# Sums of squares of an RMS norm by plain fp32 matmuls, and one weight group's sums by DMA, in a two-block FFN kernel

## The reference, cut to what matters

```python
def cond(x):        # LoRA of rank 16, one adapter per sequence, added to each of the three products
    act = silu(lora(x @ W_gate.T)) * lora(x @ W_up.T)        # 512 -> 1376
    return lora(act @ W_down.T)                              # 1376 -> 512

def ffn(y):
    nx = y * rsqrt(mean(y * y, -1) + 1e-5) * ln_w            # the norm
    return (silu(nx @ gate_w.T) * (nx @ up_w.T)) @ down_w.T  # 512 -> 1792 -> 512

out = x + ffn(cond(x))                                       # x: 8 sequences of 128 tokens, 512 features, fp32
```

## Time and profile before

| | us |
|---|---|
| median of 3 runs (395.55 to 397.08) | 396.54 |
| profiled execution, its own time | 396.24 |
| its span, first to last instruction | 394.5 |
| PE busy | 387.4 |
| DVE busy | 334.4 |
| ACT busy | 252.0 |
| POOL busy | 23.8 |

### The profile page before, as it was taken

How to read it: one execution, slowest core, us unless ns; L and a number is a source line. 1 busy time by engine, 2 the same in 40 slices (tenths; PEclk the granted TensorE clock), 3 DMA queues, 4 the chain that set the end, 5 groups by cost and what they waited for, 6 DMA issues and landing times.

```text
span 394.5 us, 5731 instructions
## 1 busy us (share of the span) xinstructions
PE 387.4 (98%) x1954; PEld 321.4 (81%) x1954; DVE 334.4 (85%) x478; ACT 252.0 (64%) x389; POOL 23.8 (6%) x25
## 2 busy tenths in 40 slices
PE   9999999999999999999899999999999999999997
PEld 5899888888888888788668888888888888888885
DVE  4799979585869889999899887878787869899994
ACT  5879886857746699994646656464646494484740
POOL 6300000000013011011100000000000000000000
PEclk9999999999999999999999999999999999999999
DMA  7540243311293997524400221313130316005112
GB/s 272 178 138 0 83 130 102 123 53 55 86 248 95 261 301 159 142 33 93 135 0 1 78 83 53 108 53 111 61 120 29 98 49 234 21 0 202 53 53 107
DMA packets 17694, 41.46 MB, mean 105 GB/s; under 512 B 2562, under 2 KB 5634, under 8 KB 17666
## 3 DMA queue, kind: packets, MB, share of 16 engines
q1 hardware_dynamic: 13792, 33.89, 25.6%
q0 software_dynamic: 2752, 5.37, 8.0%
q10 hardware_dynamic: 1122, 1.84, 1.3%
HBM read 33.75 MB, written 2.10 MB: 91 GB/s over the span
## 4 chain that ended last, share of the span: by engine, by line
PE 92%; DVE 5%; issue 1%; ACT 1%; DVEq 0%
PE bank L1631 51%; PE bank L2006 17%; PE bank L1886 10%; PE bank L1803 3%; PE bank L1849 3%; PE bank L1838 3%; PE bank L1641 3%; PE bank L1744 1%; PE bank L1797 1%; DVE nx L1353 1%; DVE xs L1074 1%; PE bank L1900 1%; ACT xs L535 1%; DVE wx L1074 1%; PE bank L2015 0%
## 5 line engine op out<-in xcount | busy, mean ns | idle before, releaser
L1631 PE MATMUL bank<-xs,ws 128*128 128x512 f32 x840 | 196.0, 390 | 1.3 <-DVE xs L1074 1.2
L1631 PEld LDWEIGHTS bank<-xs,ws 128*128 128x128 f32 x840 | 156.3, 188 | 34.5 <-ACT bank L535 1.6
L535 ACT ACTIVATE xs<-act 128x512 fp32r<-128x512 f32 (+1 forms) x72 | 49.5, 709 | 22.7 <-DVE act L1292 7.5
L1074 DVE TENSOR_TENSOR xs<-act,xs 128x512 fp32r<-128x512 f32 (+1 forms) x66 | 49.7, 766 | 3.4 <-ACT xs L535 2.8
L1074 DVE TENSOR_TENSOR ws<-wraw,ws 128x256 fp32r<-128x256 f32 (+2 forms) x45 | 30.0, 668 | 13.3 <-ACT ws L535 13.2
L535 ACT ACTIVATE bank<-bank 128x512 f32<-128x512 f32 x34 | 19.4, 578 | 34.0 <-PE bank L1631 32.4
L535 ACT ACTIVATE mu<-bank 128x512 f32<-128x512 f32 x44 | 26.1, 596 | 22.6 <-PE bank L1631 16.0
L2006 PE MATMUL bank<-xs,vs 128*128 128x512 f32 x168 | 38.2, 389 | 0.0
L2006 PEld LDWEIGHTS bank<-xs,vs 128*128 128x128 f32 x168 | 31.5, 188 | 6.5
L1074 DVE TENSOR_TENSOR ws<-wsum,ws 128x1024 fp32r<-128x1024 f32 x20 | 24.5, 1224 | 10.8 <-ACT ws L535 10.7
L535 ACT ACTIVATE ws<-wraw 128x256 fp32r<-128x256 f32 (+2 forms) x44 | 26.9, 615 | 6.9 <-PE bank L1631 3.3
(11 more groups left out here) (149 smaller groups left out, 494.5 us busy)
## 6 DMA issues: line engine op xcount, KB each, us to landing
wraw<-wgu_in SPq DMA_DIRECT2D x22, 512.0 KB, 3.3
wdr<-vs_in SPq DMA_DIRECT2D x7, 512.0 KB, 3.5
wraw<-vj_in SPq DMA_DIRECT2D x3, 896.0 KB, 4.6
act<-act POOLq DMA_DIRECT2D x4, 512.0 KB, 9.9
down_w_raw<-wc_in SPq DMA_DIRECT2D x3, 640.0 KB, 4.1
down_w_sums_raw<-wc_in SPq DMA_DIRECT2D x3, 640.0 KB, 5.1
xa<-xT_in SPq DMA_DIRECT2D x4, 256.0 KB, 4.1
xa<-xT_in ACTq DMA_DIRECT2D x2, 512.0 KB, 5.0
```

The lines of the kernel that those rows point to most:

```text
L535: return nc.scalar.activation(out_ap, in_ap, ACT.Copy, scale=scale)
L1074: return nc.vector.tensor_tensor(out_ap, raw, v32(part), ALU.subtract)
L1631: ins = mm(z[:, :], w_slot(j)[:, w, s, k * P:(k + 1) * P], xs[:, c, r, k, :], start=(start and k == 0 and s == 0 and r == 0), stop=(k == 1 ...
```

## The change

1. **Sums of squares without a split.** `sum_squares` reads `sqr` itself, with ones and the squares both taken as plain fp32, one matmul in place of two. `sum_hi`, `sum_lo`, `square_hi` and the split in `last_square` go. In half 1 both sums stand behind q1(9), no longer inside it. What waited for a split waits for the matmul (`s_nm`).
2. **Sums of set 11 by DMA.** DVE's `sums(11)` goes. SP gets `load_base(11)`, POOL `two_w(11)` and `more_w(11)`. `load_base(11)` waits for the sixth activation DMA, `T4_23`. The sums of set 12 move to a buffer in `xsum_f[:, 3]`, and `load_base(12)` waits for product 22's first low part.
3. **Work moved.** `hi_b(11)` and `lo_b(11)` move from before t1's operands to behind `square(2)` on ACT and behind `lo_c(CT1, 2)` on DVE. `copy_u3` moves ahead of t1's first operand and weights. `hi_b(12)` and `lo_b(12)` move from before the norm of half 0 to behind t1's operand of the second block (`hi_x(T_SLOT[0])`, `lo_t(1, 0)`). `scale(2)` and `scale(3)` move ahead of half 1's squares. `norm(1)`, `scale(6)` and `scale(7)` move ahead of `lo_a(13)`.

```diff
         def sums_done(j):
-            if G1 + 1 < j < G1 + 4:
-                return s_wadd, 32 * (j - G1 - 1)
-            return s_wsum, 3 * (j - 1 - (2 if j > G1 + 1 else 0))
+            if G1 < j < G1 + 4:
+                return s_wadd, 32 * (j - G1)
+            return s_wsum, 3 * (j - 1 - (3 if j > G1 else 0))
...
             def load_base(j):
-                sp.wait_ge(s_wblo, j - 2)
-                sp.dma_start(wsum[:, :, :], wbase_in[j - G1 - 2].rearrange("p (a m) -> p a m", a=4)).then_inc(s_wbase, 16)
+                if j == G1 + 2:
+                    sp.wait_ge(s_clo, KC * C22 + 2)
+                elif j == G1 + 3:
+                    sp.wait_ge(s_wblo, j - 3)
+                    sp.wait_ge(s_wbase, 32)
+                else:
+                    sp.wait_ge(s_wblo, j - 2)
+                sp.dma_start(wsum_of(j), wbase_in[j - G1 - 1].rearrange("p (a m) -> p a m", a=4)).then_inc(s_wbase, 16)
 
             load_w(G1 + 2)
+            sp.wait_ge(*t_added(T4_23))
+            load_base(G1 + 1)
+            load_w(G1 + 3)
             load_base(G1 + 2)
-            load_w(G1 + 3)
             load_base(G1 + 3)
...
-            for j in range(G1 + 2, G1 + 4):
+            for j in range(G1 + 1, G1 + 4):
                 two_w(j)
                 more_w(j)
...
-            hi_b(G1 + 1)
             hi_w10(1)
+            for i in range(2):
+                copy_u3(i)
             hi_c(CT1, 0)
             hi_w(CT1, (s_cw_add, 16))
-            for i in range(2):
-                copy_u3(i)
...
             square(2)
+            hi_b(G1 + 1)
             hi_c(CT1, 2)
...
-            sum_hi(0)
             hi_c(C22, 1)
             hi_c(C22, 2)
-            hi_b(G1 + 2)
             rsqrt(0)
...
-            sum_hi(1)
-            square_hi()
...
             lo_c(CT1, 2)
+            lo_b(G1 + 1)
             lo_w(C22)
...
             y_1(2)
+            scale(2)
+            scale(3)
             add_square(1, 1)
             add_square(1, 2)
-            sum_lo(1)
             y_1(3)
             last_square()
-            scale(2)
-            scale(3)
             lo_x(1, XF["21"], xs[:, X21, 1], nx0[:, 2:4, :], xs[:, X21, 0])
+            norm(1)
+            for m in (6, 7):
+                scale(m)
             lo_a(G1 + 3)
-            norm(1)
-            for m in (6, 7, 4, 5):
+            for m in (4, 5):
                 scale(m)
...
             def sum_squares(t, i):
-                for r in range(2):
-                    pe.wait_ge((s_sqhi, s_sqlo)[r], t + i + 1)
-                    ins = mm(N_BANK[t][:, :], ones[:, :], square_at(t, i, r),
-                             start=(i == 0 and r == 0), stop=(i == t and r == 1), skip_group_check=True)
-                ins.then_inc(s_nm, 1)
+                if i == 0:
+                    pe.wait_ge(s_acc, 3 + 2 * t)
+                else:
+                    pe.wait_ge(s_sqd, 1)
+                mm(N_BANK[t][:, :], v32(ones[:, :]), sqr[:, i, :], start=(i == 0), stop=(i == t),
+                   skip_group_check=True).then_inc(s_nm, 1)
...
             q1(S1)
             q1(S1 + 1)
+            sum_squares(1, 0)
+            sum_squares(1, 1)
             q1(S1 + 2)
```

More of the change, by code:

```diff
@@ L175, in build, with wsum_of @@
         du2 = wdr
-        def square_at(t, i, part):
-            return xs[:, (X11, XT3)[t], part, i, :]
+        def wsum_of(j):
+            return xsum_f[:, 3, :, :].rearrange("p a (b n) -> p (a b) n", n=256) if j == G1 + 2 else wsum[:, :, :]
         def act_at(f, t):
@@ L319, in build @@
         s_t, s_td = sem("td_projected"), sem("td_placed")
-        s_y, s_sq, s_sqd, s_acc, s_sqhi, s_sqlo, s_nm = (sem(n) for n in (
-            "y_ready", "squared", "last_squared", "squares_added", "square_hi", "square_lo", "square_summed"))
+        s_y, s_sq, s_sqd, s_acc, s_nm = (sem(n) for n in (
+            "y_ready", "squared", "last_squared", "squares_added", "square_summed"))
         s_ev = [sem("y_kept_half_0"), sem("y_kept_half_1")]
@@ L498, in two_w @@
             def two_w(j):
-                n = j - G1 - 2
+                n = j - G1 - 1
                 pool.wait_ge(s_wbase, 16 * n + 16)
-                nc.gpsimd.dma_start(wsum[:, 0:3, :], wmore_in[n].rearrange("p (a m) -> p a m", a=3), accum_op=ALU.add
+                if n >= 1:
+                    pool.wait_ge(s_wadd, 32 * n)
+                nc.gpsimd.dma_start(wsum_of(j)[:, 0:3, :], wmore_in[n].rearrange("p (a m) -> p a m", a=3), accum_op=ALU.add
                                     ).then_inc(s_wadd, 16)
             def more_w(j):
-                pool.wait_ge(s_wadd, 32 * (j - G1 - 2) + 16)
-                nc.gpsimd.dma_start(wsum[:, 2:4, :], wsum[:, 1:2, :].to_broadcast([P, 2, 256]), accum_op=ALU.add
+                pool.wait_ge(s_wadd, 32 * (j - G1 - 1) + 16)
+                nc.gpsimd.dma_start(wsum_of(j)[:, 2:4, :], wsum_of(j)[:, 1:2, :].to_broadcast([P, 2, 256]), accum_op=ALU.add
                                     ).then_inc(s_wadd, 16)
@@ L552, in hi_b @@
                 a.wait_ge(*sums_done(j))
-                copy(w_slot(j - 2)[:, 3:7, 0, :], wsum[:, :, :]).then_inc(s_wbhi, 1)
+                copy(w_slot(j - 2)[:, 3:7, 0, :], wsum_of(j)).then_inc(s_wbhi, 1)
             def ca(j):
@@ L570, in save @@
                 a.wait_ge(s_q1, j + 1)
-                a.wait_ge(s_sqlo, 3)
+                a.wait_ge(s_nm, 3)
                 copy(sqr[:, j % 2, :], a_bank(j)[:, :]).then_inc(s_save, 1)
@@ L804, in square @@
                 elif t == 1 and i == 0:
-                    a.wait_ge(s_sqlo, 1)
+                    a.wait_ge(s_nm, 1)
                 elif t == 1 and i == 1:
@@ L811, in square @@
                 nc.scalar.activation(to, nx[t][:, Y_ORDER[t][i], :], ACT.Square).then_inc(s_sq, 1)
[L813 to L819, removed]
             def rsqrt(t):
@@ L1032, in _ @@
             hi_x(1, T_SLOT[0], xsum_f[:, 0])
+            hi_b(G1 + 2)
             c11(S1 + 2)
@@ L1098, in lo_b @@
                 part = w_slot(j - 2)
-                sub(part[:, 3:7, 1, :], wsum[:, :, :], part[:, 3:7, 0, :]).then_inc(s_wblo, 1)
+                sub(part[:, 3:7, 1, :], wsum_of(j), part[:, 3:7, 0, :]).then_inc(s_wblo, 1)
             def c12_begin(j):
@@ L1317, in add_square @@
                 nc.vector.tensor_tensor(sqr[:, 0, :], sqr[:, 0, :], more, ALU.add).then_inc(s_acc, 1)
[L1319 to L1322, removed]
             def last_square():
@@ L1496, in _ @@
             lo_w10(0)
-            sums(G1 + 1)
             lo_w(CT4)
@@ L1501, in _ @@
             t1(0)
-            lo_b(G1 + 1)
             t1(1)
@@ L1518, in _ @@
             lo_short(1)
-            sum_lo(0)
             lo_c(C22, 1)
             lo_c(C22, 2)
-            lo_b(G1 + 2)
             norm(0)
@@ L1547, in _ @@
             lo_t(1, 0)
+            lo_b(G1 + 2)
             c11(S1 + 1)
@@ L1664, in q1 @@
                     pe.wait_ge(s_var, 2)
[L1665 to L1671, removed]
+                product(a_bank(j), j, W11, X11, True).then_inc(s_q1, 1)
             def g_prod(j):
@@ L2097 @@
         "wgu_in": blocks_of(np.concatenate([w_c, w_f], 0), [0, 1, 2, 3]),
-        "wbase_in": blocks_of(w_f[2:4], [1, 3, 2, 1]),
-        "wmore_in": blocks_of(w_f[2:4], [0, 0, 1]),
+        "wbase_in": blocks_of(w_f[1:4], [1, 3, 2, 1]),
+        "wmore_in": blocks_of(w_f[1:4], [0, 0, 1]),
         "wc_in": wd_c[:NC * P].reshape(2, KC, P, 2, 256).transpose(3, 0, 2, 1, 4).reshape(2, 2, P, KC * 256),
```

3 lines of the change are left out of this document (removed).

## The result

| | before | after |
|---|---|---|
| median | 396.35 us (395.55 to 397.38, 20 runs) | 398.19 us (396.59 to 400.14, 20 runs) |
| ratio | | 1.0047 [1.0034, 1.0061] |
| profiled execution, own time | 396.24 | 396.59 |
| its span, granted clock | 394.5, 1.000 | 394.7, 1.000 |

What follows compares the result with a forecast made beforehand. PE bounds the kernel almost everywhere; only its norm-stretch gaps can change. Gaps 4.5 before and 3.8 after, plus 1.3 more matmul work, check the chain's +0.4: 396.6 us profiled, 396.9 median, range 394.9 to 399.0.

Steps and rivals of the forecast that it cites:

- copy_u3: At 160.5 on PE: copies start at 159.1, the 0.98 gap goes, 24 matmuls start at 168.8, not 169.79.
- The first sum: PE before its first sum of squares: waits for the last add_square until 175.63, a new gap of 1.4 us.
- The price of a plain matmul: Sums of squares: a plain fp32 matmul of 512 columns costs 0.91 us, with 0.23 and 1.3 as ends.
- norm(1): Half 1's norm on DVE: rsqrt starts at 192.4 and norm(1) at 193.1, 1.6 us earlier.
- Behind it: DVE behind norm(1): lo_a(13) ends at 198.4, lo_t(1, 0) at 204.4, 0.6 early, lo_t(1, 1) at 208.4.
- The sum: p6(8) starts in effect at 208.2 where it was 207.8: +0.4 us for the whole change.
- The DMA chain: Set 11's sums by DMA: start at 151.9, 12.6 us long, there at 164.5, 3.5 us of cover before hi_b(11).
- the rival with the late chain: Set 11's DMA sums come after 168.0 and delay PE's first sum: +3.3 us at 19 us length; chance 0.10.
- PE there: PE behind norm(1): q1(11) waits 2.2 us for lo_a(13), then seven products of 1.36 bring p6(8) to 208.0.
- the band of 395.9 to 397.9: Times in us given to the main forecast of +0.4, with chance 0.55.
- dear matmuls: Rival at the three sums of squares: 1.3 us per plain matmul, +1.6 in all, 398.1 us; chance 0.10.

Runs made afterwards that it cites:

- the second comparison: The changed kernel unaltered, run again beside the kernel before on one chip: 397.19 us over 12 runs, ratio 1.0030.
- the third move: hi_b(12), lo_b(12) behind t2's operand, added to the changed kernel with lo_a(13) ahead of norm(1) and set 11's split behind the last add_square: 394.01, again 393.45 us.
- the gap alone: The kernel before with one edit, lo_a(13) moved behind scale(6) and scale(7): 399.26 us over 5 runs, ratio 1.0078.

## Why the prediction was right, and what it missed

The working at full clock held nearly step by step.

- **copy_u3.** The gap of 0.98 went, and t1's 24 matmuls start at 168.39 (168.8 said, in a program that runs 0.18 ahead of before's there). The copies start at 158.88. Put back, they cost 1.15.
- **The first sum.** The last `add_square` starts at 174.74 (174.9 said), and PE's new gap is 1.46 (1.4 said).
- **The price of a plain matmul.** From 190.31 to 193.39 stand two plain matmuls and six of the others: 3.08 - 6 x 0.227 = 1.72, 0.86 each (0.91 said; neither 0.23 nor 1.3). Where one stands alone without a wait before it (174.73 to 176.99 with six others, set 11's split moved) it costs 0.90. The price of 0.86 is 3.8 times the 0.227 step, near the four times that the length of L1744's records had given.
- **norm(1).** `rsqrt` starts at 192.22 and the norm at 192.95 (192.4 and 193.1 said).
- **Behind it.** `lo_a(13)` ends at 198.13, PE's gap is 1.92 (2.2 said), `lo_t(1, 0)` ends at 204.13 and `lo_t(1, 1)` at 208.13 (204.4 and 208.4 said). These times are 0.1 to 0.4 early, of which 0.18 is the earlier start of the stage.
- **The sum.** +0.4 said, +0.38 and +0.37 in the stages of two profiles.
- **The DMA chain.** It started at 151.81 (151.9 said). The step that failed is the length: a base of 6.0 rather than 3.7, beside the DMA of L526 that the rival had named, so about 1.2 us of cover instead of 3.5. It still held; the rival with the late chain was nearer than my 0.10 made it.
- **The missing term.** I counted a gap of PE at its own length. The step was "PE there ... a new gap of 2.2 ... seven products of 1.36 from 198.45": it takes q1(11) and the two products behind it at 0.227 per matmul. Where the clock falls, it stands at 0.50 behind this gap, and those 18 matmuls take 1.6 more; 14 executions of the first comparison have the mean clock that goes with it. By clock the difference of the medians in the 20 runs is 398.2 - 397.03 = 1.2. The fall's place is shown in the profiles of two experiments; that it is the same in the executions of after with 0.996 is inferred from putting `lo_a(13)` back, which removes both the gap and every 0.996. A second term that the working lacks is the time outside the span, 0.2.
- **What was luck.** The forecast was +0.4 and the medians say +1.8; 398.19 lies above the band of 395.9 to 397.9 that had 0.55. The range reached to 399.0 for dear matmuls and the start of a late chain, and neither came. That it held a fall of the clock is luck.

The gains and losses, from differences of the medians: plain sums -1.2 (1.35 in the stage); copies -1.5 (393.29 against 394.90, each against its own before: -2.7 and -1.2; 1.2 in the stage); set 11's split ahead of the last square +1.7 (395.55 against 393.83); `lo_b(12)` between the operands +0.4 (0.73 in the stage); `lo_a(13)` behind the scalings +1.1 at full clock (394.9, from four executions, against 393.83; 0.86 in the stage), and the clock fall 0.8 to 2.0 where it comes (398.2 against 397.03; 397.87, from three executions, against 397.04; 396.9 against 394.9). The expected gain of the first two, 2.7, was there; the placements took it back and more.

**What the stage leaves, and what is open:** the executions of after at full clock have a median of 397.03 and 397.04, 0.7 and 0.95 above before's, although the stage is only 0.38 longer. Of this, 0.2 is outside the span. In the second comparison (time less span, medians) it is 1.74 for before and 1.98 for after; every kernel in which set 11's sums come by DMA has 1.9 to 2.0, with the third move 2.1, and those without (plain sums alone, the gap alone, plain sums and copies) have 1.7 to 1.75. What makes it was not tried. The rest must lie ahead of the stage, whose start scatters by 1.3 us between the profiles; its cause is open. Some executions at full clock lie about 2 us above the others of their kernel: 399.19 has an ordinary span (395.3) and 3.9 outside it, 398.32 and 397.17 have the longer span. The profiles, of other executions, don't show why.

## What to carry to other kernels

Where one engine bounds the whole, write its gaps down before and after and ask of each new one whether it is longer than any that was there: beyond its own length it can cost the clock (here 0.50 for some 3 us behind a gap of 2.70 and, in some executions, one of 1.92; 18 matmuls then took 1.6 us more). Time a wait's own chain on the slower engines first: a dearer matmul that needs no split (0.86 us) was worth more here than cheap ones (0.227 each) with two splits ahead of them; the three sums together won 1.2 us. When several moves come together, try each alone; here two of the parts held all the gain that the time shows, and three placements nearly all the loss.

## What the runs showed of the hardware

- **A gap of PE and its clock.** With gaps up to 1.45 us (before, with all its gaps shorter, 61 executions beside the experiments; `lo_a(13)` back, with the 1.45, 12) no execution has a mean clock below 0.999. With a gap of 1.92, 14 of 20, 3 of 12 and 8 of 12 executions have 0.996. With one of 2.70, some 3 us of work behind another of 1.21, 5 of 5 have. Two profiles with 0.996 were taken, and both show the fall right behind the long gap. Fallen, the granted clock is 0.50 for some 3 us while PE is busy, and 18 matmuls take 5.97 or 5.98 us, not 4.37. The mean clock of the whole execution shows it only as 0.996.
- **A plain fp32 matmul** of 128x512 takes 0.86 to 0.90 us and stands as two records; an fp32r one takes 0.227.
- **The same base load** landed 5.6 us after its issue where it had taken 3.3 in another place of the program (6.0 and 3.7 until POOL's next DMA starts). The slow one shared full DMA engines with a DMA of L526; moving either away was not tried.
- **Time outside the span** depends on the program: 1.7 us for before and three kernels near it, 1.9 to 2.0 for after and four near it, 2.1 for the kernel with three moves. A profile's span does not show it.
